# Second attention, first sequence: the first group of heads placed by transfers on chip

## The reference, cut to what matters

```python
x = x + attn_a(layernorm(x))
x = x + ffn(layernorm(x))          # top-2 of 8 experts, and a shared expert for all tokens
x = x + attn_b(layernorm(x))       # this one
x = x + ffn(layernorm(x))

# attn_b: 16 heads of size 8, causal, with biases
qkv = encodings @ attn_W + attn_b
q, k, v = split(qkv.reshape(b, n, 16, 24).transpose(0, 2, 1, 3), 3, axis=-1)
scores = einsum('bhki,bhqi->bhkq', k, q) / sqrt(8)
prob = softmax(where(mask, scores, -10000), axis=2)
out = einsum('bhkq,bhkl->bhql', prob, v) ... @ out_W + out_b
```

## Time and profile before

| what | value |
|---|---|
| runs, us | 773.38, 774.40, 777.24; median 774.4 |
| profiled execution, us | 779.2 |
| its span, first to last instruction, us | 777.5 |
| TensorE busy | 708.2 us, 91% of the span |
| VectorE / ScalarE / GpSimd busy | 68% / 58% / 58% |
| mean granted TensorE clock | 0.975 of full |
| transfers | 89.38 MB, mean 115 GB/s |
| store to `qk_rows`, from issue to landing | 3.9 us median of 16 |
| loads from `qk_rows` into `qc`, from issue to landing | 2.9 us median |

### The profile page before, as it was taken

The page is one execution under the profiler, slowest core; times in us unless marked ns, Lnnn a source line. Parts: engine busy times, 40 slices in busy tenths (PEclk is TensorE's granted clock), DMA queues, the critical chain, the costliest instruction groups (busy, mean ns, idle before and its releaser), DMA issues. The chain is left out here.

```text
span 777.5 us, 18451 instructions
## 1 busy us (share of the span) xinstructions
PE 708.2 (91%) x6152; PEld 643.6 (83%) x6152; DVE 525.9 (68%) x1665; ACT 449.7 (58%) x1144; POOL 454.4 (58%) x564
## 2 busy tenths in 40 slices
PE   6888789699999997888999998999999899999996
PEld 5777689699999995666777776777779799999996
DVE  5877775366556555867888989877777356665536
ACT  2566454244444443676878878787755344446545
POOL 7367777166666662334545776777767166666650
PEclk9999989899999998899999999999999899999999
DMA  7997111455556335233433444323101346555318
GB/s 252 313 317 171 45 48 55 57 109 109 103 98 129 80 96 135 92 98 109 148 90 98 124 124 140 94 92 121 53 30 52 50 75 135 110 92 114 91 60 290
DMA packets 167718, 89.38 MB, mean 115 GB/s; under 512 B 120576, under 2 KB 151890, under 8 KB 167528
## 3 DMA queue, kind: packets, MB, share of 16 engines
q1 hardware_dynamic: 156792, 70.02, 36.3%
q0 software_dynamic: 9216, 17.34, 6.6%
q10 hardware_dynamic: 1616, 0.84, 0.6%
HBM read 49.63 MB, written 39.67 MB: 115 GB/s over the span
## 5 line engine op out<-in xcount | busy, mean ns | idle before, releaser
L1289 ACT ACTIVATE hT<-bank,bias_T 128x256 f32<-128x256 f32 x448 | 175.7, 475 | 193.5 <-PE bank L917 193.4
L624 POOL DMA_INDIRECT y_rows<-yo,row_cur x160 | 168.7, 1054 | 124.3 <-DVE yo L1828 88.9
L1934 DVE TENSOR_REDUCE negp<-bank 128x2 f32<-128x512 f32 (+1 forms) x192 | 129.6, 685 | 45.6 <-PE bank L979 27.2
L938 PE MATMUL bank<-w_s,hT 128*128 128x128 f32 x1280 | 156.0, 275 | 0.0
L609 POOL DMA_INDIRECT x_slots<-xr,slot_u x128 | 131.4, 1026 | 41.6 <-issue 34.3
L938 PEld LDWEIGHTS bank<-w_s,hT 128*128 128x128 f32 x1280 | 150.0, 192 | 0.0
L917 PE MATMUL bank<-xT_hl,w_hl 128*128 128x256 f32 x960 | 136.5, 292 | 10.8 <-DVE xT_hl L1702 10.7
L693 POOL TENSOR_SCALAR_AFFINE_SELECT pt<-pt 128x512 f32<-128x512 f32 x128 | 86.0, 680 | 92.6 <-ACT pt L1372 92.3
L917 PEld LDWEIGHTS bank<-xT_hl,w_hl 128*128 128x128 f32 x960 | 122.0, 194 | 13.2 <-issue 11.6
L1372 ACT ACTIVATE pt<-bank 128x512 f32<-128x512 f32 x192 | 107.8, 596 | 40.6 <-PE bank L1000 38.7
L1828 DVE TENSOR_TENSOR yo<-bank,b_b 128x256 f32<-128x256 f32 x80 | 34.0, 425 | 103.8 <-PE bank L938 102.2
(11 more groups left out here) (214 smaller groups left out, 1209.4 us busy)
## 6 DMA issues: line engine op xcount, KB each, us to landing
xg_all<-x_slots SPq DMA_DIRECT2D x320, 32.0 KB
w_s<-in_L_ffn_w SPq DMA_DIRECT2D x32, 256.0 KB
qk_rows<-qks SPq DMA_DIRECT2D x16, 512.0 KB, 3.9
bdk<-qk_rows SPq DMA_DIRECT2D x187, 32.0 KB
qc<-qk_rows SPq DMA_DIRECT2D x45, 128.0 KB, 2.9
x_slots<-xg_all SPq DMA_DIRECT2D x1, 5440.0 KB, 21.2
y_rows<-xg_all SPq DMA_DIRECT2D x1, 4096.0 KB, 14.3
yab<-y_rows SPq DMA_DIRECT2D x16, 256.0 KB, 3.5
```

Source lines behind the costliest of these rows:

```text
L624: pool.indirect_dma_start(y_rows, bass.IndirectOffsetOnAxis(ap=row_cur[:, g % ROWS, j:j + 1], axis=0), yo[:, g % RING, j, :], None, bounds ...
L938: m = pe.matmul(yb(w, l)[:, j * P:(j + 1) * P], hT[:, w % 2, f, j * P:(j + 1) * P], wt[:, f, :], start=(f == 0), stop=(f == FT - 1))
L1289: a = act.activation(hT[:, w % 2, f, :], HB[2 * (w % 2) + f // 2][:, (f % 2) * 256:(f % 2) * 256 + 256], ACT.Silu, bias=bias_T[:, b0 + f:b ...
L1934: dve.tensor_reduce(dst, AB[(g + k) % 2][:, :].rearrange("p (j k) -> p j k", j=heads), AX.X, ALU.max, negate=True).then_inc(S.amax_done, 1)
```

## The change

The first group of the first sequence (U = 0) no longer goes through memory. Fifteen transfers, 12 of 8 partitions and 1 KB each into `bdk` and 3 of 32 partitions and 1 KB each into `qc`, copy it from `qks` to its places on chip (`first_group`). SP issues seven of them, behind the mask's and before it waits for the store; ScalarE waits for `hilo_done` and issues the other eight, ahead of the four activations of the expert layer's last piece. They count, with the mask rows, on a semaphore of their own (`first_in`), for which U = 0 waits. The loads through memory take groups 1 to 3 only (24 KB and 96 KB instead of 32 and 128), and U = 1 waits for them. `q_loaded` keeps the counts: for parity 0 the mask's transfer of the first sequence now counts elsewhere, so its counts are lower by 16. Nothing else changes, and the other fifteen sequences go as before.

```diff
+        def q_loaded(t, par):
+            return 64 * t + (64 if par else 48)
...
+        def first_group(eng, k):
+            if k < 12:
+                part, j = divmod(k, 4)
+                dst, src = bdk[32 * part + HD * j:32 * part + HD * j + HD, 0, 0, j, :], qks[HD * j:HD * j + HD, 0, part % 2, 1, :]
+            else:
+                part = k - 12
+                dst, src = qc[32 * part:32 * part + 32, 0, 0, :], qks[0:32, 0, part // 2, 0, :]
+            eng.dma_start(dst.bitcast(F32), src.bitcast(F32)).then_inc(S.first_in, 16)
...
@@ restack (SP) @@
-                need(sp, q_in, 64 * t)
+                if t > 0:
+                    sp.wait_ge(q_in, q_loaded(t - 1, par))
                 sp.dma_start(qk_rows[par], qks[:, par, :, :, :].bitcast(F32)).then_inc(rows_stored, 16)
...
-                sp.dma_start(qc[96:P, par, :, :]..., mask_rows...).then_inc(q_in, 16)
+                sp.dma_start(qc[96:P, par, :, :]..., mask_rows...).then_inc(S.first_in if n == 0 else q_in, 16)
+                if n == 0:
+                    for k in range(BY_SP):
+                        first_group(sp, k)
                 sp.wait_ge(rows_stored, 16 * t + 16)
...
+                g0 = 1 if n == 0 else 0
-                        sp.dma_start(bdk[32 * part + r:32 * part + r + HD, par, :, j, :].bitcast(F32), rows[r:r + HD, :, half, 1, :]
+                        sp.dma_start(bdk[32 * part + r:32 * part + r + HD, par, g0:GRP, j, :].bitcast(F32), rows[r:r + HD, g0:GRP, half, 1, :]
@@ pass1 (TensorE) @@
-                    if g == 0:
-                        pe.wait_ge((S.qc_in0, S.qc_in1)[par], 64 * t + 64)
+                    if U == 0:
+                        pe.wait_ge(S.first_in, 16 * 16)
+                        pe.wait_ge(S.key_mask_in, 16 * 2)
+                    elif g == 0 or U == 1:
+                        pe.wait_ge((S.qc_in0, S.qc_in1)[par], q_loaded(t, par))
                         pe.wait_ge((S.bdk_in0, S.bdk_in1)[par], 16 * 12 * (t + 1))
-                        if U == 0:
-                            pe.wait_ge(S.key_mask_in, 16 * 2)
@@ first_rows (ScalarE) @@
-                    act.dma_start(bdk[..., 0, :, j, :].bitcast(F32), rows[HD * j:HD * j + HD, :, part % 2, 1, :]).then_inc(S.bdk_in0, 16)
+                    act.dma_start(bdk[..., 0, 1:GRP, j, :].bitcast(F32), rows[HD * j:HD * j + HD, 1:GRP, part % 2, 1, :]).then_inc(S.bdk_in0, 16)
-                    act.dma_start(qc[32 * part:32 * part + 32, 0, :, :].bitcast(F32), rows[:, :, part // 2, 0, :]).then_inc(S.qc_in0, 16)
+                    act.dma_start(qc[32 * part:32 * part + 32, 0, 1:GRP, :].bitcast(F32), rows[:, 1:GRP, part // 2, 0, :]).then_inc(S.qc_in0, 16)
@@ attn_b_pair (ScalarE) @@
                         if i == -1 and h == 0 and g == 2:
+                            act.wait_ge(S.hilo_done, 1)
+                            for k in range(BY_SP, 15):
+                                first_group(act, k)
                             silus(0, ITEMS - 1)
                             first_rows()
```

More of the change, by code:

```diff
@@ L253, in build @@
         S.xg_used = sem("xg_used")
+        S.first_in = sem("first_in")
         S.row_set = sem("row_set")
@@ L424, in restack @@
                 need(sp, k_in, 16 * 12 * t)
-                need(sp, q_in, 64 * t)
+                if t > 0:
+                    sp.wait_ge(q_in, q_loaded(t - 1, par))
                 sp.dma_start(qk_rows[par], qks[:, par, :, :, :].bitcast(F32)).then_inc(rows_stored, 16)
                 need(sp, S.c_done, 3 * GRP * (n - 1))
-                sp.dma_start(qc[96:P, par, :, :].bitcast(F32).rearrange("p g (a q) -> p (g a) q", a=2), mask_rows.unsqueeze(1).broadcast_to([32, 2 * GRP, P])).then_inc(q_in, 16)
+                sp.dma_start(qc[96:P, par, :, :].bitcast(F32).rearrange("p g (a q) -> p (g a) q", a=2), mask_rows.unsqueeze(1).broadcast_to([32, 2 * GRP, P])
+                             ).then_inc(S.first_in if n == 0 else q_in, 16)
+                if n == 0:
+                    for k in range(BY_SP):
+                        first_group(sp, k)
                 sp.wait_ge(rows_stored, 16 * t + 16)
                 rows = qk_rows[par].rearrange("(g r) a b t -> r g a b t", g=GRP)
+                g0 = 1 if n == 0 else 0
                 for part, half in enumerate((0, 1, 0)):
@@ L1342, in first_rows @@
                     part, j = divmod(k, 4)
-                    act.dma_start(bdk[32 * part + HD * j:32 * part + HD * j + HD, 0, :, j, :].bitcast(F32),
-                                  rows[HD * j:HD * j + HD, :, part % 2, 1, :]).then_inc(S.bdk_in0, 16)
+                    act.dma_start(bdk[32 * part + HD * j:32 * part + HD * j + HD, 0, 1:GRP, j, :].bitcast(F32),
+                                  rows[HD * j:HD * j + HD, 1:GRP, part % 2, 1, :]).then_inc(S.bdk_in0, 16)
                 for part in range(3):
-                    act.dma_start(qc[32 * part:32 * part + 32, 0, :, :].bitcast(F32), rows[:, :, part // 2, 0, :]).then_inc(S.qc_in0, 16)
+                    act.dma_start(qc[32 * part:32 * part + 32, 0, 1:GRP, :].bitcast(F32), rows[:, 1:GRP, part // 2, 0, :]).then_inc(S.qc_in0, 16)
             def bt_copy(t, par):
```

## The result

The changed kernel takes 782.72 us (median of 6 runs, 779.05 to 784.93) against 775.21 (6 runs, 773.38 to 777.24): ratio 1.0091, 95% interval 1.0064 to 1.0117, that is +7.1 us, 5.0 to 9.1. The prediction was 774.1 in a range of 771.5 to 776.9, with 0.95 on no change. It was wrong.

A forecast was written before the change was run, and what follows sets the result against it. TensorE, busy 91% of a 777.5 us span, was taken as the bound. Memory wait -1.8 and push of the chain by ScalarE's issues +1.5 gave -0.3: 778.9 profiled, 774.1 as a median, range 771.5 to 776.9.

The forecast's parts named there:

- ScalarE's eight issues: On-chip issues ahead of the last expert piece's activations: 3.0 us, between 2.7 and 3.4, taken from ScalarE's query-load issues.
- The push through the chain: Activations 2.4 us later delay TensorE's second products, the transpose and its copy (1.5 later); first group starts at 309.3.
- ScalarE's second eight issues: ScalarE's loads through memory: begin when the activations end at 302.7, take 3.07 us, end at 305.8, then the copy.
- The norm: Next pair's normalization shifts 2.2 us, in time by 0.2 for its transpose; U1 can't start over 0.5 earlier.
- rival (a): TensorE's clock stays up from 305 to 315 in the second attention's start: -1.5 us, 772.9; chance 0.2.
- Rival (b): TensorE's idle before the last second products drops the clock, that run takes 3.1 us: +0.8, 775.2; chance 0.27.
- U1's and U4's transfers: Loads for later groups and the second sequence land in time; U1's wait hidden by 0.6 at the worst.
- SP's part: SP's seven small transfers behind the mask's take 298.86 to 301.2; 0.1 us, hidden by its wait for stored rows.
- The cap of 1.8 us: Most the aim can bring: first group starting at about 307.8 instead of 309.57, 0.23% of the time.
- here the trace does not agree: Against a page's rule that issue time is usually small: ScalarE's eight issues take 3.07 us, as long as a landing.
- The sign and the chances: Whole kernel: about -0.3 us, cases between -1.8 and +1.2; chances: same 0.95, faster 0.02, slower 0.03.
- issues on ScalarE stall: Listed as making the prediction wrong: an issue like SP's longest, 1.63 us, would push the whole chain by 1.3.

The follow-up runs named there:

- src_mem: Changed kernel with the fifteen first-group transfers reading a zeroed stretch of device memory instead of on-chip rows; +4.0 us against the kernel before (1.7 to 6.3).
- after_busy20: Changed kernel with twenty idle identity matmuls in TensorE's hole before the last second products; +6.8 us against the kernel before (4.6 to 9.2).
- extra4: Kernel before with four unneeded on-chip transfers issued by ScalarE ahead of its four activations; +1.2 us against the kernel before (-0.5 to 2.9).
- pool8: Changed kernel with ScalarE's eight first-group transfers issued by GpSimd instead; +0.4 us against the kernel before (-1.0 to 1.8).
- after_again: Second series of the changed kernel, nothing altered; ratio 1.0101 against the kernel before (1.0063 to 1.0139), +7.8 us.
- before_2: Kernel before, unaltered, run once more for a second profile; profiled execution 776.24 us.
- extra8: Kernel before with eight unneeded on-chip transfers issued by ScalarE ahead of its four activations; +5.1 us against the kernel before (2.8 to 7.4).
- silus_first: Changed kernel with ScalarE's four activations placed ahead of its eight on-chip issues; +5.0 us against the kernel before (3.2 to 6.9).
- after: The changed kernel itself, first series and profile, against the kernel before; 782.72 us, ratio 1.0091.
- pool8_split: Changed kernel with GpSimd issuing the eight and ScalarE copying the next transpose before its last three loads; +1.0 us against the kernel before (-0.5 to 2.5).
- after_busy: Changed kernel with forty idle identity matmuls in TensorE's hole before the last second products; +9.9 us against the kernel before (7.4 to 12.5).
- pool8_best: Changed kernel with GpSimd issuing the eight, ScalarE's transpose copy earlier, and VectorE's combining moved into idle time; -1.9 us against the kernel before (-3.4 to -0.3).

## Why the prediction was wrong, point by point

- **"On-chip transfers of this shape are not in the trace; the nearest rows are ScalarE's own eight issues"**: this is the step that failed. The term for ScalarE's eight issues, 3.0 us with a high end of 3.4, measured 5.86. The row of line 464 shown above was in the trace, has both ends on chip, and gives 8 x 0.65 = 5.2; even the nearest row was outside my range. I had taken the shape (8 or 32 partitions) for what makes rows near, and it was the kind of the two ends.
- **The push through the chain**: with 5.8 in place of 3.0 my own steps give a copy at 308.5 instead of 305.8 (nothing of the push is absorbed any more: the transpose is done at 308.4, when ScalarE's second eight issues end too) and U0 at 312.0, 2.4 later than before. Measured: 3.3 later. That this is near is in part luck: two errors of the chain cancel. The copy came 12.3 us after the split, not 10.5, mostly because the second run took 3.45 us instead of 2.03; but from the copy to the end of the bias it took 2.47 us, not the 3.47 that I had kept, because the clock was up by then. In src_mem, with the eight at 3.39, my steps give U0 0.1 later than before; it is 0.6 earlier or 0.3 later by the two profiles, and there too copy to bias took 2.47.
- **ScalarE's second eight issues, put behind the end of the activations (302.7)**: wrong, without effect. The issue of the first load begins 0.1 us after the start of the first activation (305.24 and 305.36), so they run beside them.
- **The norm, "not a price for this forecast, but a floor"**: named, but with 0.2 us to spare I should have carried it as a price wherever the clock stays up, as in rival (a). In src_mem TensorE was ready for the transpose 13.2 us after the split (my steps at that issue cost: 13.8) and the normalization ended at 14.0 (13.6). The wait was 0.91 us in src_mem and in the changed kernel, where U1 is 4.4 later than before while U0 is 3.3 later.
- **Rival (b), the hole drops the clock**: right in kind. With a hole of 2.4 to 3.0 us the second run stayed at 2.02; with 5.1 to 5.4 it took 3.45 to 3.75, against 3.1 in my working. Its share is 1.5 to 2.5 us at U4 by after_busy20. My price of +0.8 had the clock in it but the wrong hole.
- **Rival (a), the clock stays up**: in src_mem and extra4 the granted clock is 1.00 from 300 to 310, against 0.51 in the earlier trace rows, as (a) says; but from 310 to 315 it was 0.64 and 0.71, after the next waits. In src_mem the gain was gone by U4; extra4's U4 is within the two of before (24.59 against 24.72 and 24.33).
- **U1's and U4's transfers**: right. Neither waited for a transfer after the change.
- **SP's part, "hidden by that wait"**: mis-sized like ScalarE's, without effect. SP's seven issues took 5.19 us instead of 2.3, so its loads began at 305.36, 3 us later after the split than before, where I had put 0.1. It cost nothing that shows: pool8 has them too (4.81 us).
- **The cap of 1.8 us**: not exceeded by anything that moves only the transfers: pool8 puts U0 1.5 earlier and shows no gain in the time. That the best version gains 1.9 is a coincidence; it moves the copy and the combining too, so the cap doesn't bind it, and its U0 is 3.2 earlier.
- **"here the trace does not agree"** (on the cost of an issue): that compared unlike things, eight issues together (3.07 us) with the landing of one transfer (2.9). One issue was 0.38 us there, an eighth of a landing, and on chip 0.73. What makes issues dear is their number in one engine's order.
- **The sign and the chances**: I wrote "no case comes near" 3.9 us. All cases were built on one issue cost between 2.7 and 3.4; a single mis-sized term moved all of them together. That issues on ScalarE stall stood among what would make it wrong, as single ones of 1.63 us, and no case with a chance had it; what came was all eight at 0.73.

**What stays open.** U4 is 5.3 to 5.7 us later, the time 7.1 to 7.8 with intervals from 4.9 up. The 1.5 to 2 us between are within these intervals; the profiled executions do not show a place for them. Of the 6.7 us between the profiled executions of after_again and before_2, 5.6 lie ahead of U4 and 1.3 behind U63, where the profiles of one and the same code differ by 1.1 (219.05 and 217.9 us). For extra8 the two agree (5.0 and 5.1), for silus_first they do not (2.8 and 5.0). And why the issue of an on-chip transfer costs twice as much is not known from these runs; they vary the source, the engine and the neighbours, and no more.

## What to carry to other kernels

Before moving an issue onto a compute engine, look up what an issue of that kind costs, and take "kind" by where both ends are, not by size: a row from a far part of the trace with the same two ends is nearer than one a microsecond away with others. An issue ahead of an activation delays whoever waits for that activation by its whole length, here 5.86 us for eight; the same eight issues on an engine that idles there cost nothing that could be measured (+0.4, -1.0 to 1.8). And a chain that is "in time by 0.2 us" is the next bound, so the gain behind it has to be counted only up to there.

## What the runs showed of the hardware that I had not expected

- An issue with both ends on chip took 0.60 to 0.86 us on ScalarE and SP as a rule. Single ones took longer: 2.0 to 2.1 us at line 464's place in after, extra4 and pool8_split, and 1.4 to 1.9 in after_busy and after_busy20. With one end in memory it was about 0.32 for 8 partitions. The number of partitions (8 or 32) made little difference on chip (medians 0.67 and 0.71 on ScalarE). GpSimd issued the same eight in 0.50 to 0.67 us each.
- Issues took longer beside another engine's on-chip issues: SP's seven loads took 3.58 us beside ScalarE's in extra8, against 2.34, and ScalarE's five took 2.62 beside SP's and GpSimd's in pool8, against 1.79:

```profile
301.73 3.58 SPq L441 DMA_DIRECT2D bdk<-qk_rows  x7
```

```profile
298.33 2.62 ACTq L1369 DMA_DIRECT2D bdk<-qk_rows  x5
```

- VectorE's combining of four tiles took 1.92 us in pool8_split, where GpSimd's addition of 1.27 us ran over it, and 1.13 in pool8_best, where it ran ahead:

```profile
303.03 1.92 DVE L1951 SCALAR_TENSOR_TENSOR x<-yab,gate,x 128x128 f32<-128x128 f32 x4
```

The Trainium skill, page "SBUF — State Buffer", section "SBUF: two separate sides", says that a VectorE instruction with two inputs in SBUF and a GpSimd instruction that reads SBUF block each other, the second until the first is done; by that rule the trace agrees: GpSimd's addition ran from 302.73 to 304.00, and of the four combining instructions that began at 303.03 the first took 1.13 us and the others 0.34; the median of all 64 in that profile is 0.35.
